# Loading a transposed activation by DMA instead of transposing it on TensorE, in a gated cross-attention with routed experts

## The reference, cut to what matters

```
xn = layernorm(x)                                   # x: (8, 512, 512)
Q_char, K_sub, V_sub = xn @ Wq_c.T + bq_c, ctx @ Wk_s.T + bk_s, ctx @ Wv_s.T + bv_s
char2sub = softmax(Q_char @ K_sub.T * scale) @ V_sub
Q_sub, K_char, V_char = ctx @ Wq_s.T + bq_s, xn @ Wk_c.T + bk_c, xn @ Wv_c.T + bv_c
sub2char = softmax(Q_sub @ K_char.T * scale) @ V_char
gate = sigmoid(concat(char2sub, sub2char) @ Wg.T + bg)
x1 = x + tanh(g_xattn) * (gate * char2sub + (1 - gate) * sub2char)
n1 = layernorm(x1); probs = softmax(n1 @ router_w + router_b)
out = x1 + tanh(g_ffn) * max(probs) * (n1 @ expert_w[argmax] + expert_b[argmax])
```

## Time and profile before

| | |
|---|---|
| median of 3 runs | 1125.27 us |
| the profiled execution's own time | 1130.69 us |
| its span, first to last instruction | 1129.0 us |
| TensorE, busy | 1109.5 us, 98% |
| TensorE's weight loads, busy | 913.0 us, 81% |
| vector engine, busy | 707.9 us, 63% |
| scalar engine, busy | 446.2 us, 40% |
| GpSimd, busy | 203.6 us, 18% |
| mean granted TensorE clock | 0.997 |

### The profile page before, as it was taken

The page is one execution under the profiler, slowest core; times in us unless marked ns, Lnnn a source line. Parts: engine busy times, 40 slices in busy tenths (PEclk is TensorE's granted clock), DMA queues, the critical chain, the costliest instruction groups (busy, mean ns, idle before and its releaser), DMA issues.

```text
span 1129.0 us, 17281 instructions
## 1 busy us (share of the span) xinstructions
PE 1109.5 (98%) x5615; PEld 913.0 (81%) x5615; DVE 707.9 (63%) x1490; ACT 446.2 (40%) x808; POOL 203.6 (18%) x325
## 2 busy tenths in 40 slices
PE   8999999999999999999999999999999999997998
PEld 7878888888888888888888888888888888786776
DVE  7867645665656564656466556645665656986565
ACT  6345323442434243434343334323442444652432
POOL 2000100210112010200021001100110101176564
PEclk9999999999999999999999999999999999999999
DMA  8332211221112110211021102110210232685774
GB/s 299 112 114 75 63 50 38 60 76 36 57 22 65 65 74 19 69 65 74 9 78 65 49 25 78 60 51 37 59 65 20 93 114 66 210 252 175 192 249 127
DMA packets 63138, 99.00 MB, mean 88 GB/s; under 512 B 20122, under 2 KB 20662, under 8 KB 63096
## 3 DMA queue, kind: packets, MB, share of 16 engines
q1 hardware_dynamic: 52928, 72.64, 20.2%
q0 software_dynamic: 7264, 19.20, 5.4%
q10 hardware_dynamic: 2904, 6.63, 1.6%
HBM read 71.15 MB, written 29.12 MB: 89 GB/s over the span
## 4 chain that ended last, share of the span: by engine, by line
PE 94%; issue 2%; SPq 1%; DVE 1%; another core or an unknown queue 1%; ACT 1%; DMA 0%; POOL 0%; POOLq 0%; ACTq 0%; DVEq 0%
PE mm L163 60%; PE u L1082 16%; PE u L163 8%; PE tr L1034 5%; PE tr L163 1%; PE mm L1892 1%; PE u L437 1%; PE tr L1126 1%; SPq L1641 1%; PE mm L483 0%; SPq L1642 0%; DVE arena L1314 0%; DMA pairs_as_f<-in_L_ffn_expert_b 0%; DVE mx L1333 0%
## 5 line engine op out<-in xcount | busy, mean ns | idle before, releaser
L163 PE MATMUL mm<-arena 128*128 128x512 f32 x1512 | 361.5, 392 | 1.6 <-DVE arena L1314 1.6
L163 PEld LDWEIGHTS mm<-arena 128*128 128x128 f32 x1512 | 280.8, 188 | 59.1 <-DVE arena L1314 1.8
L1082 PE MATMUL u<-arena 128*128 128x512 f32 x768 | 188.9, 396 | 0.0
L163 PE MATMUL mm<-arena,q_pair 128*128 128x512 f32 x768 | 180.1, 392 | 0.0
L163 PEld LDWEIGHTS mm<-arena,q_pair 128*128 128x128 f32 x768 | 142.7, 188 | 30.3 <-issue 0.5
L1082 PEld LDWEIGHTS u<-arena 128*128 128x128 f32 x768 | 140.7, 188 | 28.1
L1314 DVE TENSOR_TENSOR arena<-mm,arena 128x512 fp32r<-128x512 f32 x65 | 45.0, 692 | 98.8 <-ACT arena L1183 94.7
L1183 ACT ACTIVATE arena<-mm 128x512 fp32r<-128x512 f32 x64 | 38.3, 599 | 145.3 <-PE mm L163 145.3
L1188 ACT ACTIVATE probs<-mm,neg_top 128x512 f32<-128x512 f32 x64 | 44.2, 690 | 117.1 <-DVE neg_top L1337 115.8
L1179 ACT ACTIVATE q_pair<-mm,c_col 128x512 fp32r<-128x512 f32 x62 | 42.6, 689 | 116.0 <-PE mm L163 113.5
L163 PE MATMUL mm<-c2s_pair,arena 128*128 128x512 f32 x360 | 87.1, 391 | 0.0
(11 more groups left out here) (254 smaller groups left out, 1503.7 us busy)
## 6 DMA issues: line engine op xcount, KB each, us to landing
slot_as_f<-in_ctx_by_columns SPq DMA_DIRECT2D x8, 1024.0 KB, 5.4
in_tile<-in_ctx SPq DMA_DIRECT2D x31, 256.0 KB, 2.6
x_rows<-x_tile SPq DMA_DIRECT2D x29, 256.0 KB
in_tile<-in_x SPq DMA_DIRECT2D x28, 256.0 KB, 2.7
slot_as_f<-in_x_by_columns SPq DMA_DIRECT2D x7, 1024.0 KB, 5.4
x_rows_early<-x_tile SPq DMA_DIRECT2D x28, 256.0 KB, 2.3
slot_as_f<-in_L_ffn_expert_w SPq DMA_DIRECT2D x4, 1024.0 KB, 5.3
pairs_as_f<-in_L_ffn_expert_b SPq DMA_DIRECT2D x16, 256.0 KB
```

Of the source, the lines that this page charges most:

```text
L163: last = pe.matmul(bank, lhsT(a, c), rhs(b, c), start=start and n == 0, stop=stop and n == C * len(PASSES) - 1)
L1082: last = pe.matmul(u_bank[m][:], v_pair[:, i % 2, a, tile(m)], pt_pair[:, i % 2, p], start=i == 0 and n == 0, stop=i == T - 1 and n == 2)
```

## The change

x's columns no longer come from transposes of the normalised rows from batch 1 on. SP loads the raw columns of x from DRAM (1 MB a batch) into the low half of x's slot in the arena. The scale and shift of the 512 rows are stored to a small DRAM tensor (two DMAs of 256 pieces of 8 bytes), and loaded back as one row broadcast to all 128 partitions (4 KB, 512 KB written), which goes to the half of a slot that PT used. The vector engine then multiplies the columns by the scale row and adds the shift row (XA, 8 operations a batch), and scalar and vector engine split them into the pair (XB), all around the gate products. Batch 0 keeps its transposes.

The rows of x are still normalised (XN), since XD reads them. Statistics of four tiles are kept until they are stored, so `mv_x` gets a second tensor for tiles 2 and 3. XS 1 to 3, XN 1 to 3, XD 1 to 3 and CD 3 stand at other places of the list. The waits on XT ahead of x's and ctx's loads are gone.

In the work of the batch before, the transposes M 3 go behind the fourth score product, the logits LG 0 behind the first value product, and MX 3, BS 1, NT 2 and LG 0 shift with them. `bn_1` is gone, BS uses `bn_x`.

```diff
@@ steps_of_a_batch
-        s += cur("Q", 0, 3) + prev("NT", 1) + prev("BS", 1) + prev("M", 2) + prev("M", 3)
-        s += cur("S", 0, 0) + prev("NR", 0) + cur("S", 0, 1) + prev("MX", 2)
-        s += cur("S", 0, 2) + prev("MX", 3) + prev("NR", 1) + cur("S", 0, 3) + prev("LG", 0) + cur("NP", 0, 3)
+        s += cur("Q", 0, 3) + prev("NT", 1) + prev("M", 2)
+        s += cur("S", 0, 0) + prev("BS", 1) + prev("NR", 0) + cur("S", 0, 1) + prev("MX", 2)
+        s += cur("S", 0, 2) + prev("NR", 1) + cur("S", 0, 3) + prev("M", 3) + cur("NP", 0, 3)
-    s += prev("NT", 2) + prev("BS", 2) + cur("V", 0, 0) + opened("AE12") + prev("LG", 1) + cur("PT", 0, 0) + opened("AE13")
+    s += prev("MX", 3) + prev("BS", 2) + cur("V", 0, 0) + opened("AE12") + prev("LG", 0) + prev("LG", 1) + cur("PT", 0, 0)
+    s += opened("AE13") + prev("NT", 2)
-    s += nxt("XT", 0) + load(8) + cur("PT", 1, 0) + load(9)
-    s += cur("V", 1, 1) + load(10) + nxt("CD", 3) + late(15) + cur("PT", 1, 1) + table(1) + load(11, 12) + cur("U", 1, 0)
-    s += load(13) + nxt("CT", 0) + nxt("XS", 1)
-    s += cur("V", 1, 2) + load(14) + nxt("XN", 1) + cur("PT", 1, 2) + table(2) + load(15) + cur("U", 1, 1) + nxt("CT", 1)
-    s += nxt("XS", 2) + nxt("XD", 1)
+    s += load(8) + nxt("XS", 1) + cur("PT", 1, 0) + load(9) + nxt("XN", 1) + nxt("CD", 3)
+    s += cur("V", 1, 1) + load(10) + late(15) + cur("PT", 1, 1) + table(1) + load(11, 12) + cur("U", 1, 0)
+    s += load(13) + nxt("XD", 1) + nxt("CT", 0) + nxt("XS", 2)
+    s += cur("V", 1, 2) + load(14) + nxt("XN", 2) + cur("PT", 1, 2) + table(2) + load(15) + cur("U", 1, 1) + nxt("CT", 1)
+    s += nxt("XS", 3) + nxt("XD", 2)
-    s += cur("V", 1, 3) + fetch(4, 5) + nxt("XN", 2) + nxt("XT", 1) + cur("PT", 1, 3) + cur("U", 1, 2)
-    s += nxt("CT", 2) + nxt("XS", 3) + prev("ID", 0) + nxt("XD", 2) + nxt("XT", 2) + nxt("XN", 3)
+    s += cur("V", 1, 3) + fetch(4, 5) + nxt("XN", 3) + cur("PT", 1, 3) + cur("U", 1, 2)
+    s += nxt("CT", 2) + prev("ID", 0) + nxt("XD", 3)
-    return s + cur("G", 0, 0) + nxt("XD", 3) + nxt("XT", 3) + cur("G", 0, 1) + cur("G", 0, 2) + cur("G", 0, 3)
+    for i in range(C):
+        s += nxt("XA", i)
+    return (s + cur("G", 0, 0) + nxt("XB", 0) + nxt("XB", 1) + cur("G", 0, 1) + nxt("XB", 2) + nxt("XB", 3)
+            + cur("G", 0, 2) + cur("G", 0, 3))
@@ sync
         def after_x(b, t):
-            await_count(sp, waits_passed_sp, xt_tr, per_batch(b, t))
             await_count(sp, waits_passed_sp, x_dotted, per_batch(b, t))
+        def load_columns_of_x(b):
+            of_batch = x_stats_dram[bass.ds(b * L, L), :]
+            await_count(sp, waits_passed_sp, x_scaled, 4 * b + 4)
+            for n, of_tiles in enumerate((mv_x, mv_x_rest)):
+                to = x_stats_dram[bass.ds(b * L + n * (L // 2), L // 2), :].rearrange("(t p) s -> p t s", p=P)
+                sp.dma_start(to, of_tiles[:, :, 1:3], allow_slow_non_contiguous=True).then_inc(xs_stored, 16)
+            await_count(sp, waits_passed_sp, v_mm, per_dir(b - 1, 1, T - 1))
+            sp.dma_start(k.slot_as_f32[XT][:, LO], x_columns[bass.ds(b, 1)].rearrange("o (c p) l -> p (o c) l", p=P)
+                         ).then_inc(xc_loaded, 16)
+            await_count(sp, waits_passed_sp, xs_stored, 32 * b)
+            await_count(sp, waits_passed_sp, u_mm, per_dir(b - 1, 1, C - 1))
+            sp.dma_start(xs_rows.rearrange("p l s -> p (l s)"), of_batch.rearrange("l s -> (l s)").partition_broadcast(P)
+                         ).then_inc(xc_loaded, 16)
...
             load_rest_of_x(b + 1)
+            load_columns_of_x(b + 1)
             load_residual(b)
@@ scalar
+                elif kind == "XB":
+                    act.wait_ge(xc_ready, per_batch(bb - 1, i))
+                    act.activation(arena[:, XT, HI, i], columns_of_x(i), ACT.Copy).then_inc(xt_hi, 1)
@@ vector
+                elif kind == "XA":
+                    if i == 0:
+                        dve.wait_ge(xc_loaded, 32 * bb)
+                    raw = columns_of_x(i)
+                    then(dve.tensor_tensor(raw, raw, scale_rows, ALU.mult))
+                    dve.tensor_tensor(raw, raw, shift_rows, ALU.add).then_inc(xc_ready, 1)
+                elif kind == "XB":
+                    dve.wait_ge(xt_hi, per_batch(bb, i))
+                    low(arena[:, XT, LO, i], columns_of_x(i), arena[:, XT, HI, i]).then_inc(xt_lo, 1)
@@ vector, XS
-                        dve.wait_ge(x_normed, per_batch(bb, i) - 2)
+                        dve.wait_ge(x_normed, per_batch(bb, i) - T)
+                        if not here_first:
+                            dve.wait_ge(xs_stored, 32 * (bb - 1))
```

More of the change, by code:

```diff
@@ L82, in gated_attention_and_experts @@
     x1_early = nc.dram_tensor("x1_rows_early", (N - L, ROWX), F32, kind="Internal").ap()
+    x_stats_dram = nc.dram_tensor("x_row_statistics", (N, 2), F32, kind="Internal").ap()
     list_dram = nc.dram_tensor("token_lists", (SLOTS, LINE), I32, kind="Internal").ap()
@@ L128, in gated_attention_and_experts @@
         with ExitStack() as scope:
-            attention = attention_part(nc, scope, top, k, x_rows, c_rows, x_columns, ctx_columns, x1_dram, x1_early, list_dram,
-                                       expert_w, (Wv_s_columns, Wv_c_columns, Wg_columns[0:H, :],
+            attention = attention_part(nc, scope, top, k, x_rows, c_rows, x_columns, ctx_columns, x_stats_dram, x1_dram, x1_early,
+                                       list_dram, expert_w, (Wv_s_columns, Wv_c_columns, Wg_columns[0:H, :],
                                                   Wg_columns[H:2 * H, :]), weights)
@@ L600, with attention_part @@
 EXPERT_ORDER = (A_X, WV_S, A_C, CT, XT, WV_C, PAIRS, WG_C)
-def attention_part(nc, scope, top, k, x_rows, c_rows, x_columns, ctx_columns, x1_dram, x1_early, list_dram, expert_w,
-                   late_weights, weights):
+def attention_part(nc, scope, top, k, x_rows, c_rows, x_columns, ctx_columns, x_stats_dram, x1_dram, x1_early,
+                   list_dram, expert_w, late_weights, weights):
     arena, ident, ones_bf, before_bf = k.arena, k.ident, k.ones_bf, k.before_bf
@@ L626, in attention_part @@
     row_next = sb("row_next", [P, 2, T])
-    bn_1 = sb("bn_1", [P, 6])
     stats_flat = sb("stats", [P, 4 * T + LINE - 4])
@@ L641, in attention_part @@
     slot_i = sb("slot_i", [P, T], I32)
+    mv_x_rest = sb("mv_x_rest", [P, 2, 3])
     kept = (normed[:], diff[:], normed_t[:].rearrange("p n c t -> p (n c t)").bitcast(F32), x1_tile[:, 1])
@@ L674, in attention_part @@
     x_scaled, x1_scaled = sem("x_scaled"), sem("x1_scaled")
+    xc_loaded, xs_stored, xc_ready = sem("xc_and_xs_loaded"), sem("xs_stored"), sem("xc_ready")
     x_stats, x_normed, x_dotted, c_dotted = sem("x_stats"), sem("x_normed"), sem("x_dotted"), sem("c_dotted")
@@ L743, in x_stat_of, with columns_of_x @@
             return weights.first_stats[:, t]
-        return mv_x[:, t % 2]
+        return (mv_x if t < 2 else mv_x_rest)[:, t % 2]
+    def columns_of_x(i):
+        return k.slot_as_f32[XT][:, LO, i]
+    xs_rows = k.slot_as_f32[PAIRS][:, HI, 0:2].rearrange("p c l -> p (c l)").rearrange("p (l s) -> p l s", s=2)
+    shift_rows, scale_rows = xs_rows[:, :, 0], xs_rows[:, :, 1]
     def keys_of(d):
@@ L970, in sync @@
         load_rest_of_x(1)
+        load_columns_of_x(1)
         load_residual(0)
@@ L1422, in run @@
                         dve.wait_ge(stats_copied, 16 * bb + 16)
-                    bn_ready(dve.bn_stats(bn_1[:], x1))
-                    dve.bn_aggr(stats[:, i, 0:2], bn_1[:]).then_inc(x1_stats, 1)
+                    bn_ready(dve.bn_stats(bn_x[:], x1))
+                    dve.bn_aggr(stats[:, i, 0:2], bn_x[:]).then_inc(x1_stats, 1)
                     dve.wait_ge(x1_stats, per_batch(bb, i))
@@ L1575, in attention_part @@
     part.x1_copied, part.stats_copied = x1_copied, stats_copied
-    part.tiles_read = (xt_tr, x_dotted, c_dotted)
+    part.tiles_read = (x_dotted, c_dotted)
     part.x1t_done, part.probs = x1t_done, probs
@@ L1582, in attention_part @@
     return part
-DVE_LINKS = 43
+DVE_LINKS = 47
 POOL_LINKS = 16
```

## The result

The changed kernel takes 1117.08 us (median of 4 runs, 1116.53 to 1117.92) against 1125.66 for the kernel before in the same comparison; the ratio is 0.9927, with a 95% interval of 0.9914 to 0.9939. That is 8.6 us or 0.7% faster, by the interval 6.9 to 9.7 us; 8.2 were forecast. The profiled execution took 1117.25 us.

The account below looks back on a forecast made before the run. TensorE's own work, 94% of the span, was taken as the bound. Six loop batches gain 1.35 us each (8.1), batch 0 nothing, batch 7 0.1: 8.2 us, so the median of 1125.27 becomes 1117.1, range 1112 to 1122.

Parts of the forecast that it names:

- The transposes: TensorE, batches 1 to 7: four XT groups removed, 0.44 us each, 1.75 a batch, 12.2 us if nothing waits.
- The prediction's list of times: Second direction's value products: starts worked out from V(1,0)'s end at 463.11 to U(1,3), which can start at 481.55.
- The wait that took their place: XN waits for XS and GpSimd, delaying casts; about 0.4 us a loop batch given back at U(1,3).
- The 0.1 at PT(1,1): TensorE before PT(1,1), behind XS 1 and PT(1,0)'s subtraction: just met, up to 0.1 us lost a batch.
- The move: M 3 behind S(0,3), LG 0 behind V(0,0): 0.1 us gained a batch, seven times; PT(0,0)'s 0.63 stays.
- XA: Vector engine, gate stretch: eight operations, 5.8 us a batch, starting 6 us after U(1,3)'s end, costing nothing.
- The limit of 10.6 us: Gate stretch: if XA's inputs came 10.6 us or later after U(1,3)'s end, every further microsecond would be one of time.
- the slower case: Statistics broadcast lands late and XA with it; slower from 11.8 us after U's end, 1134 at 13 us; chance 0.07.
- The 8-byte stores: Statistics stores to DRAM: 2.6 us to landing, before the broadcast is wanted.
- The third case: GpSimd held up under CD 3 by 0.4 to 0.75 us, or XS 1 later: 1119.5 to 1122; chance 0.2.
- Batch 0: Late weights and XS 1 delay PT(1,1); 0.4 us lost at U(1,3), XT 3 returns 0.44: nothing gained.
- Case 2: The wait cascade doesn't bite and only batch 0 gives back: 11.5 to 12.9 us gained, 1112.3 to 1113.8; chance 0.2.

Follow-up runs that it names:

- the chain moved away and the split wait: Changed kernel with XN 1-3 behind casts, XS 1 and batch 0's late weights behind PT(1,0), PT(d,0) awaiting its last quarter separately: 1110.82 us, ratio 0.9872.
- XN behind: Changed kernel with XN 1, 2 and 3 each put behind the casts of PT(1,1), PT(1,2), PT(1,3), and XD 1 behind XS 2: 1112.90 us, ratio 0.9891.
- XD 2: Changed kernel with only XD 2 moved from right behind XS 3 to behind V(1,3)'s subtraction: 1113.68 us, ratio 0.9895.
- the two runs: M 3, MX 3, BS 1, LG 0, NT 2 moved alone in the kernel before: 1123.82 us; put back in the changed kernel: 1117.20 us.
- three broadcasts in turn: Changed kernel with two whole 512 KB statistics broadcasts, each waited for, ahead of the real one: 1135.02 us, ratio 1.0087.
- The combined run: Changed kernel with XN 1-3 behind the casts, XD 1 behind XS 2, XS 1 and batch 0's late weights behind PT(1,0): 1112.59 us, ratio 0.9884.

## Why the prediction was right, point by point

**The transposes.** 0.44 us a group, as the rows had it. Three of the four (XT 0, 1 and 2) stood between V(1,0) and U(1,3), where the new chain became the path, so they were not worth 0.44 each: the stretch became 0.77 us shorter (22.30 to 21.53) and not 1.31. The prediction's list of times had that right, since it took U(1,3)'s start from the chain and not from the sum of groups. The kernel with the chain moved away and the split wait gets the whole 1.32 (20.98).

**The wait that took their place.** Forecast 18.44 us from V(1,0)'s end to U(1,3), measured 18.50; given back at U(1,3) 0.4 a batch, measured 0.3. Taking the chain away (XN behind) or shortening it (XD 2) returned 0.3 a batch. The 0.1 at PT(1,1) did not occur, no wait is there in the loop. Not foreseen was PT(1,0)'s 0.07 + 0.19 us: XT 0 had covered the end of the normalisation. The trace of before shows it in batch 7, which has no XT, with 0.07 us of issue ahead:
```profile
937.33 0.63 PE tr L1034 x4
```
It cost nothing only because the chain was longer. With it, TensorE's own work up to U(1,3) was about 18.5 us and not 18.2, as long as the chain, so the two losses, 0.26 and 0.28, add up to the 0.54 that the stretch gave back; 0.5 was forecast, from other parts. That this total fits is in part luck.

**The move.** Sized at 0.1 a batch; the two runs give 0.22 and 0.24. The missing part is PT(0,0)'s wait for the last quarter of the probabilities (0.12 + 0.13 us), which the prediction said would stay. It read the 0.63 in the earlier trace rows as a property of following logits; these leave it at 0.49 to 0.50. This is the term that was mis-sized most.

**XA.** Free, as forecast. It started 6.4 us after U's end in batch 3 and 6.0 to 7.0 over all batches, forecast 6, and 1.33 us a pair instead of 1.45. The broadcast took longer than 4.6 (6.2 from issue to XA, behind x's columns; 4.2 when it was issued after them). The limit of 10.6 us lies between 10.7 and 11.3 by the runs, and was crossed only by three broadcasts in turn, and then the slower case's mechanism worked as described, with gate product 3 as a second place.

**The 8-byte stores.** Sized at 2.6 us to landing, from the row of 4-byte words, and said to land before the broadcast is wanted. The changed kernel's DMA view has a median of 4.2 and 4.1 us for the two, and in batches 4, 5 and 6 of the seven the broadcast waited for the second one: it was issued 0.68, 1.08 and 0.45 us after U(1,3)'s end, 0.10 to 0.15 in the others. The second store of batch 5 was issued at 711.91 and its broadcast at 717.31. SP's wait for it, over the whole execution (us in total, times, longest):
```profile
SPq L174 <- DMA x_row_statistics<-mv_x_rest: 23.1, 7, 4.1
```
So this step was wrong, and it cost no time, since XA had over 3 us to spare. Whether the length comes from the small pieces or from x's columns, issued 0.6 us behind, no run here shows.

**GpSimd.** The pow was not slowed under CD 3, and the first operation was under XD 2. The third case fell with it. The Trainium skill ("SBUF — State Buffer", two separate sides) has the lock held by whoever starts first. The trace agrees as far as the pow goes, which started 0.04 us ahead of CD 3, and with 0.68 beside XD 2 against 0.22 away from it. It doesn't show the other half: CD 3, which started second, took 0.74 us, as XD 1 did with no GpSimd operation beside it.

**Batch 0.** Forecast nothing gained. It lost 0.56 us ahead of its gate and got back the 0.44 of XT 3 behind it. The combined run shows both causes: the chain (1.0 us, 47.64 to 46.63), and XS 1 with the late weights ahead of PT(1,0)'s low part (1.1 us, to 45.55).

**The sum.** 6 x 1.50 for 6 x 1.35, 0.29 of batch 7's own for 0.1, -0.12 for 0: 9.2 for 8.2, with the errors in the move (+1.0 over seven batches) and in the small waits. The 5 us by which the profile of before lay over its median stood behind the last gate, outside the change; carrying them over unchanged was right. The median of 1117.08 against the forecast 1117.1 is closer than the terms: the kernel before took 1125.66 and not 1125.27 in the comparison, and the profiles give 9.2 us where the medians give 8.6. Case 2's sum is 11.2 to 12.7 by its own terms, not 11.5 to 12.9, which changes nothing here.

## What to carry to other kernels

Before counting removed work at its full price, write down the next chain that spans the same stretch, start by start from the rows; here it was 18.4 us long by the forecast against 18.2 of remaining work, and it alone told what three of the four groups were worth. A matmul group that takes longer than its equals (0.63 for 0.44) can be a wait, even where no idle time is shown: look for what ended just ahead of it. Where an in-order engine mixes evictions on which TensorE depends with side work that waits for a slower engine, put the side work behind the eviction; and a group that needs its last input only for its last part can wait for it there.

## What the runs showed of the hardware that was not expected

The total time could not resolve 1.7 us in one case: with the move undone each loop batch was 0.24 us longer, and the medians were 1117.20 and 1117.08; the stretch behind the last gate varied from 165.5 to 167.4 us between the profiles of kernels that are the same there.

The same 512 KB broadcast, in the run with three in turn, took 4.3 to 6.0 us where 1 MB had been issued some 4 us before it, 3.3 to 3.9 as the second, with nothing beside it, and 4.0 to 4.5 as the third, where 1 MB was issued 0.6 us behind it.

A TensorE group whose input comes just in time shows little or no idle time and takes longer: four transposes 0.63 us for 0.44 (PT(1,0)), twelve matmuls 3.02 to 3.06 for 2.75 (U(1,3)).

For the rows of x, GpSimd's first operation took 0.66 to 0.69 us wherever it started some 0.16 us after an XD or CD (the kernel before, the changed one, XN behind, combined), and 0.22 to 0.25 otherwise; the pow that started 0.04 us ahead of one kept its 0.57.
